# Attention heads of a conditioned sequence model: value bias moved to GpSimd, a PSUM bank for each head tile, two of four normalising products on GpSimd

## The reference

```
x1  = layernorm(x) * (scale1 + 1) + shift1
qkv = x1 @ mat_qkv_w.T + concat(q_bias, 0, v_bias)        # 16 heads of 16 columns
q   = q / max(norm(q), 1e-12) * exp(min(scale_mul, log 100))
k   = k / max(norm(k), 1e-12)
o   = softmax(q @ k.T) @ v
x   = x + (o @ proj_w.T + proj_b) * gamma1                # then a second MLP
```

## Time and profile before

| | |
|---|---|
| median of 3 runs | 3158.72 us (3158.28 to 3159.21) |
| the profiled execution's own time | 3156.91 us |
| its span in the profile | 3155.1 us |
| PE busy | 3087.0 us (98%) |
| DVE busy | 2740.4 us (87%) |
| ACT busy | 2711.8 us (86%) |
| POOL busy | 2483.4 us (79%) |

### The profile page before, as it was taken

The page is one execution under the profiler, slowest core; times in us unless marked ns, Lnnn a source line. Parts: engine busy times, 40 slices in busy tenths (PEclk is TensorE's granted clock), DMA queues, the critical chain, the costliest instruction groups (busy, mean ns, idle before and its releaser), DMA issues.

```text
span 3155.1 us, 59484 instructions
## 1 busy us (share of the span) xinstructions
PE 3087.0 (98%) x23304; PEld 2634.1 (83%) x23304; DVE 2740.4 (87%) x2985; ACT 2711.8 (86%) x4528; POOL 2483.4 (79%) x638
## 2 busy tenths in 40 slices
PE   8999999999999999999999999999999999999999
PEld 6998899895699889988389988998848998888965
DVE  2999999986499999997659999999666999999963
ACT  4999999974699999995579999999458999999845
POOL 2999999981299999996139999999416999999910
PEclk9999999999999999999999999999999999999999
DMA  5222223210222222222022222222102222222100
GB/s 180 85 84 69 84 68 96 76 56 29 69 68 83 74 91 76 83 85 66 1 80 71 86 82 77 81 78 88 46 16 79 83 82 82 75 71 81 58 14 8
DMA packets 195240, 225.70 MB, mean 72 GB/s; under 512 B 77448, under 2 KB 149640, under 8 KB 193680
## 3 DMA queue, kind: packets, MB, share of 16 engines
q1 hardware_dynamic: 194960, 221.89, 22.8%
HBM read 217.37 MB, written 4.48 MB: 70 GB/s over the span
## 4 chain that ended last, share of the span: by engine, by line
PE 65%; POOL 20%; issue 7%; ACT 4%; DVE 2%; DMA 1%; SPq 0%; DVEq 0%; POOLq 0%; ACTq 0%
PE bank L1140 17%; POOL states L680 13%; PE bank L1120 12%; PE bank L1020 9%; PE bank L1121 7%; POOL y_gated L680 6%; PE bank L1365 4%; PE bank L1116 3%; PE bank L1402 2%; PE bank L1505 2%; PE bank L1390 2%; ACT decay L865 1%; ACT inflow_tok L856 1%; PE bank L1196 1%; PE bank L1293 1%
## 5 line engine op out<-in xcount | busy, mean ns | idle before, releaser
L680 POOL TENSOR_TENSOR states<-states,c_rows 128x2048 f32<-128x2048 f32 x336 | 1532.0, 4577 | 120.5 <-DVE states L1648 118.1
L1648 DVE TENSOR_TENSOR_SCAN states<-decay,bank 128x512 f32<-128x512 f32 x1376 | 1580.6, 1202 | 38.7 <-PE bank L1121 14.2
L865 ACT ACTIVATE decay<-dt,a_log 128x512 f32<-128x512 f32 x2048 | 1309.0, 717 | 0.0
L856 ACT ACTIVATE inflow_tok<-dtx_tok,b_tok 128x512 f32<-128x512 f32 x1536 | 998.0, 719 | 62.9 <-PE bank L1121 40.2
L1120 PE MATMUL bank<-ident,inflow_tok 128*128 128x128 f32 x5280 | 898.7, 279 | 20.0 <-DVE states L1648 7.6
L1140 PE MATMUL bank<-ident,states 128*128 128x128 f32 x5504 | 826.9, 273 | 10.5 <-POOL states L680 6.2
L1648 DVE TENSOR_TENSOR_SCAN y_gated<-decay,bank 128x512 f32<-128x512 f32 x672 | 776.0, 1201 | 13.0 <-ACT decay L865 2.8
L680 POOL TENSOR_TENSOR y_gated<-y_gated,c_rows 128x2048 f32<-128x2048 f32 x168 | 768.8, 4576 | 15.7 <-DVE y_gated L1648 14.5
L1120 PEld LDWEIGHTS bank<-ident,inflow_tok 128*128 128x128 f32 x5280 | 604.6, 140 | 174.4 <-issue 60.7
L1121 PE MATMUL bank<-b_diag,dtx_tok 128*128 128x128 f32 x3520 | 680.9, 275 | 0.0
L1140 PEld LDWEIGHTS bank<-ident,states 128*128 128x128 f32 x5504 | 643.3, 141 | 21.5 <-POOL states L680 14.2
(11 more groups left out here) (174 smaller groups left out, 2583.1 us busy)
## 6 DMA issues: line engine op xcount, KB each, us to landing
c_rows<-c_spill SPq DMA_DIRECT2D x256, 512.0 KB, 3.7
b_diag<-diag_ring SPq DMA_DIRECT2D x256, 128.0 KB, 2.4
xproj_w<-in_xproj_w SPq DMA_DIRECT2D x32, 320.0 KB, 4.2
in_w<-in_in_w SPq DMA_DIRECT2D x16, 512.0 KB, 4.6
out_w<-in_out_w SPq DMA_DIRECT2D x4, 1024.0 KB, 8.3
in_w<-in_fc_w SPq DMA_DIRECT2D x8, 512.0 KB, 4.1
xproj_w<-in_w SPq DMA_DIRECT2D x8, 512.0 KB, 4.6
xproj_w<-in_fc_w SPq DMA_DIRECT2D x4, 1024.0 KB, 4.8
```

The source lines that it names most:

```text
L680: pool.tensor_tensor(state_row, state_row, c_row.to_broadcast([P, KI, L]), ALU.mult).then_inc(weighed, PAIRS)
L856: last_tok = act.activation(inflow_tok[:, r % SLOTS, t, :], dtx_tok[:, d, t, :], ACT.Copy, scale=b_tok[:, d, t, s:s + 1])
L865: act.activation(decay[:, r % SLOTS * KI + k, :], dt[:, d, k, :], ACT.Exp, scale=a_neg[:, d, k, s:s + 1]).then_inc(decay_ready, 1)
L1648: dve.tensor_tensor_scan(state_slots[r % STATES][:, k, time], decay[:, slot, time], banks[k % INFLOW_BANKS][:, time], 0.0, ALU.mult, ALU.a ...
```

## The change

- PE: the four head tiles get a bank each (4, 5, 0, 1), so no tile waits for a reader of its bank; the turns of tiles 1, 2 and 3 stand one ahead of each head tile; the bias matmuls of the values are gone.
- ACT: the squares of a tile come ahead of the copy of its keys, tile 0's stand ahead of the shift of tile 3, and keys are squared straight from PSUM as before.
- DVE: the maximum and the scale become one instruction with two tensor inputs (`norm_over`), with the inverse scale, and the reciprocal follows it; the products of tiles 2 and 3 stay on DVE.
- POOL: the products of tiles 0 and 1, and two instructions that add the value bias in place to two tiles each, once ACT has copied them; its wait for `qk_unit` ahead of L729 is gone.
- PE waits for the value bias (`v_biased`) ahead of the first product with the values.

```diff
-QK_BANK = 4
+QK_BANKS = (4, 5, 0, 1)
+POOL_TILES = 2
...
+                for t in range(POOL_TILES):
+                    pool.wait_ge(k_ready, b * TT + t + 1)
+                    pool.wait_ge(norm_inv_ready, b * TT + t + 1)
+                    pool.tensor_tensor(heads(qk_pad[:, t, :, :].rearrange("p g c -> p (g c)"), LANE)[:, :, 0:HD],
+                                       heads(qk[:, t, :], HD), norm_inv[:, t, :].unsqueeze(2).to_broadcast([P, 2 * H, HD]),
+                                       ALU.mult).then_inc(qk_unit, 1)
+                for i in range(2):
+                    values = v_ones[:, 2 * i:2 * i + 2, :, 0:HD]
+                    pool.wait_ge(v_ready, b * 2 + i + 1)
+                    pool.tensor_tensor(values, values, heads(row_b[:, V_BIAS, :], HD).unsqueeze(1).to_broadcast([P, 2, H, HD]),
+                                       ALU.add).then_inc(v_biased, 1)
                 pool.wait_ge(res_ready, (b * 2 + 1) * TT)
-                pool.wait_ge(qk_unit, (b + 1) * TT)
                 pool.tensor_tensor(proj_g, proj_w[:], gate[:, GAMMA1, :].unsqueeze(1).to_broadcast([P, KD, D]),
...
+            def square(b, t):
+                bank = banks[QK_BANKS[t]]
+                act.wait_ge(q_ready, b * TT + t + 1)
+                act.activation(qk_sq[:, t, D:2 * D], bank[:, D:2 * D], ACT.Square)
+                act.activation(qk_sq[:, t, 0:D], qk[:, t, 0:D], ACT.Square).then_inc(sq_ready, 1)
+                act.activation(qk[:, t, D:2 * D], bank[:, D:2 * D], ACT.Copy).then_inc(k_ready, 1)
...
+                square(b, 1)
+                head_root(0)
+                square(b, 2)
+                head_root(1)
+                square(b, 3)
+                head_root(2)
+                head_root(3)
...
+                ln_turn(b, 2, 1)
+                heads_tile(0)
+                ln_turn(b, 2, 2)
+                heads_tile(1)
+                ln_turn(b, 2, 3)
+                heads_tile(2)
+                heads_tile(3)
...
-                    pe.matmul(to, ident[0:1, 0:1].to_broadcast([1, P]), row_b[0:1, V_BIAS, :], start=True, stop=False,
-                              skip_group_check=True)
...
+                def invert(t):
+                    dve.wait_ge(norm_ready, b * TT + t + 1)
+                    dve.scalar_tensor_tensor(norm_over[:, t, :], norm[:, t, :], EPS_NORM, inv_scale[:], ALU.max,
+                                             ALU.mult).then_inc(norm_over_ready, 1)
+                    dve.wait_ge(norm_over_ready, b * TT + t + 1)
+                    dve.reciprocal(norm_inv[:, t, :], norm_over[:, t, :]).then_inc(norm_inv_ready, 1)
...
+                query(0)
+                query(1)
+                sum_squares(0)
+                query(2)
+                sum_squares(1)
+                invert(0)
+                query(3)
+                sum_squares(2)
+                invert(1)
+                sum_squares(3)
+                invert(2)
+                unit(2)
+                invert(3)
+                unit(3)
```

More of the change, by code:

```diff
@@ L184, in build @@
         scale_cap = sb("scale_cap", [P, H])
-        qk_scale = sb("qk_scale", [P, 2 * H])
+        inv_scale = sb("inv_scale", [P, 2 * H])
         proj_w = sb("proj_w", [P, KD, D])
@@ L249, in build @@
         norm = norm_sq
-        norm_max = norm_sq
+        norm_over = norm_sq
         norm_inv = b_diag[:, HALF + 1, :].rearrange("p (t h) -> p t h", t=TT)
@@ L294, in build @@
         cap_ready = sem("cap_ready")
-        q_scale_ready = sem("q_scale_ready")
+        inv_scale_ready = sem("inv_scale_ready")
         mod_mm = sem("mod_mm")
@@ L379, in build @@
         k_ready = sem("k_ready")
+        v_biased = sem("v_biased")
         v_ready = sem("v_ready")
@@ L383, in build @@
         norm_ready = sem("norm_ready")
-        norm_max_ready = sem("norm_max_ready")
+        norm_over_ready = sem("norm_over_ready")
         norm_inv_ready = sem("norm_inv_ready")
-        qk_inv_ready = sem("qk_inv_ready")
         qk_unit = sem("qk_unit")
+        qk_unit_high = sem("qk_unit_high")
         qk_turned = sem("qk_turned")
@@ L426, in build, with heads @@
         out_rows = out.rearrange("b (t p) d -> b p t d", p=P)
+        def heads(row, e):
+            return row.rearrange("p (h e) -> p h e", e=e)
         def lead_last(bank):
@@ L628, in _ @@
             pool.memset(ring_zeros, 0.0).then_inc(zeros_ready, 1)
-            pool.memset(qk_scale[:, H:2 * H], -1.0).then_inc(sign_ready, 1)
+            pool.memset(inv_scale[:, H:2 * H], -1.0).then_inc(sign_ready, 1)
             pool.memset(minus_half[:], -0.5).then_inc(half_ready, 1)
@@ L780, in ln @@
                 eps_of = eps[:, 0:1] if i == 1 else eps[:, 1:2]
[L781 to L787, removed]
                 root(0)
@@ L790, in ln @@
                 shift(0)
+                if i == 2:
+                    root(2)
+                    shift(1)
+                    root(3)
+                    shift(2)
+                    square(b, 0)
+                    shift(3)
+                    return
                 shift(1)
@@ L875, in _ @@
                     act.wait_ge(sign_ready, 1)
-                    act.activation(qk_scale[:, 0:H], scale_cap[:], ACT.Exp).then_inc(q_scale_ready, 1)
+                    act.activation(inv_scale[:, 0:H], scale_cap[:], ACT.Exp, scale=-1.0).then_inc(inv_scale_ready, 1)
                 prepare(0, 0, s)
@@ L906, in batch, with head_root @@
                 ln(b, 2)
-                def root(t):
+                def head_root(t):
                     act.wait_ge(norm_sq_ready, b * TT + t + 1)
                     act.activation(norm[:, t, :], norm_sq[:, t, :], ACT.Sqrt).then_inc(norm_ready, 1)
[L912 to L919, removed]
+                square(b, 1)
[5 more added lines that the diff above has]
+                head_root(3)
                 act.wait_ge(ones_ready, b + 1)
@@ L1295, in batch, with heads_tile @@
                     last.then_inc(res_mm, 1)
-                ln_turn(b, 2, 1)
-                for t in range(TT):
+                def heads_tile(t):
                     ln_wait(b, 2, t)
-                    pe.wait_ge(res_ready, (b * 2 + 1) * TT + t + 1)
                     if t > 1:
-                        pe.wait_ge(k_ready, b * TT + t - 1)
+                        pe.wait_ge(res_ready, (b * 2 + 1) * TT + t - 1)
                     for kc in range(KD):
-                        last = pe.matmul(banks[QK_BANK + t % 2], h_t[:, kc, t * P:(t + 1) * P], qkv_w[:, kc, 0:2 * D],
+                        last = pe.matmul(banks[QK_BANKS[t]], h_t[:, kc, t * P:(t + 1) * P], qkv_w[:, kc, 0:2 * D],
                                          start=(kc == 0), stop=(kc == KD - 1))
                     last.then_inc(qk_mm, 1)
-                    if t == 0:
-                        ln_turn(b, 2, 2)
-                        ln_turn(b, 2, 3)
+                ln_turn(b, 2, 1)
[5 more added lines that the diff above has]
+                heads_tile(3)
                 def value_tile(t):
                     to = banks[V_BANK + t // 2][:, t % 2 * D:(t % 2 + 1) * D]
-                    pe.matmul(to, ident[0:1, 0:1].to_broadcast([1, P]), row_b[0:1, V_BIAS, :], start=True, stop=False,
-                              skip_group_check=True)
                     for kc in range(KD):
-                        last = pe.matmul(to, h_t[:, kc, t * P:(t + 1) * P], qkv_w[:, kc, 2 * D:3 * D], start=False,
+                        last = pe.matmul(to, h_t[:, kc, t * P:(t + 1) * P], qkv_w[:, kc, 2 * D:3 * D], start=(kc == 0),
                                          stop=(kc == KD - 1), skip_group_check=True)
@@ L1328, in turn_heads @@
                         for t in range(TT):
-                            pe.wait_ge(qk_unit, b * TT + t + 1)
+                            if t < POOL_TILES:
+                                pe.wait_ge(qk_unit, b * POOL_TILES + t + 1)
+                            else:
+                                pe.wait_ge(qk_unit_high, b * (TT - POOL_TILES) + t - POOL_TILES + 1)
                             last = pe.transpose(banks[TURN_BANK + i][:, t * P:(t + 1) * P], qk_pad[:, t, i * NG + g, :], ident[:])
@@ L1396, in weigh @@
                     pe.wait_ge(probs_t_ready, b * UNITS + (j + 1) * HG)
+                    if j == 0:
+                        pe.wait_ge(v_biased, (b + 1) * 2)
                     if g and kt == 0:
@@ L1720, in sum_squares, with query @@
                                       ALU.add).then_inc(norm_sq_ready, 1)
-                def unit(t):
+                def query(t):
+                    dve.wait_ge(qk_mm, b * TT + t + 1)
+                    dve.tensor_tensor(qk[:, t, 0:D], banks[QK_BANKS[t]][:, 0:D], row_b[:, Q_BIAS, :], ALU.add).then_inc(q_ready, 1)
+                def invert(t):
                     dve.wait_ge(norm_ready, b * TT + t + 1)
[L1724 to L1733, removed]
@@ L1738, in batch @@
                     dve.wait_ge(sign_ready, 1)
[L1739 to L1748, removed]
```

(8 more changed lines are left out.)

2 lines of the change are left out of this document (1 added, 1 removed).

## The result

The changed kernel takes 3173.06 us (median of 5 runs, 3169.43 to 3179.32) against 3158.28 for the kernel before on the same chip (5 runs, 3154.53 to 3159.21): a ratio of 1.0052, 95% interval 1.004 to 1.0065. It is slower, by some 15 us. That lies inside the range of 3144 to 3176, and outside the forecast's own range of 3154 to 3165. The profiled execution took 3173.06 us, with a span of 3171.3.

A forecast was written before the change was run, and what follows sets the result against it. It took PE's chain from the MLP's residual to the first score, with DVE close behind, as the bound. PE's 3.5 us a batch less 4.1 us of waits gave +0.8 us: 3158.72 + 0.8 = 3159.5, own range 3154 to 3165, full 3144 to 3176.

The forecast's parts named there:

- rival 4: POOL beside DVE: one more POOL step lost than placed, or steps of 1.9 to 2.35 us; +7 to +17 us; chance 0.16.
- The forecast's own sum: Stretch before the first score, four batches: fair turns, POOL steps of 1.27 us; +0.8 us, giving 3159.5; chance 0.33.
- the collisions: DVE's two-input guard steps and products wait for POOL's SBUF reads: 4.1 us of waits, eating the 3.5 us gained.
- A: Stretch from tile 0's heads to the first score; last transposes forecast 0.2 us later, times four +0.8 us.
- PE's own gain: PE's heads and values before the first score: 3.5 us a batch, 2.5 from the bias matmuls, the rest the stall.
- Rivals 1 and 2: DVE beside POOL: no holding-up that matters, 3145, chance 0.15; or only large products wait, guard steps slip through, 3148, chance 0.17.
- Rival 3: POOL keeps its turn through back-to-back instructions, delaying DVE's product 3 by 13.6 us a batch; +50 us, 3209; chance 0.19.
- whole-instruction hold: A two-SBUF-input DVE instruction and a SBUF-reading POOL instruction block each other for a whole instruction; 3.10 against 0.68 us.
- PE's clock: PE's pause before the scores may shift when its clock falls: at most some 1 us a batch, +-4 us.
- B: Attention from first score to the last pair turning its output rows; 73.38 and 72.61 us before, only the clock varying it.

The follow-up runs named there:

- e1: Changed kernel plus seven spare matmuls in PE's wait ahead of the first turned heads, POOL left as it is; 3157.46 us, ratio 1.0001.
- e6: Kernel before with only the value bias moved to POOL behind all head products, plus five spare matmuls in PE's wait; 3157.62 us, ratio 1.0001.
- e4: Kernel before with only the bias matmuls removed and POOL adding the value bias behind all head products; no spare matmuls; 3175.45 us, ratio 1.0045.
- e8: Changed kernel with all four products on DVE, POOL's value bias behind them, four spare matmuls in PE's wait; 3147.05 us, ratio 0.9974.
- e2: Changed kernel with POOL's value bias held back until DVE's products of tiles 2 and 3 are done; 3151.04 us, ratio 0.9983.
- e5: Changed kernel with POOL's value bias held back behind DVE's products, plus three spare matmuls in PE's remaining wait; 3147.97 us, ratio 0.9969.

## Why the prediction came out as it did

**The range held by luck.** The time lies inside 3144 to 3176 only because rival 4 stretched the upper end to 3176, for slower or further POOL steps, and those didn't come. The forecast's own sum, with its 4 us for the clock, missed.

**Right: the collisions eat what PE gains.** The forecast said that A would change by +0.2 us a batch, +0.8 in all; it changed by +0.7. That the two numbers stand so near is luck. The waits on DVE came to 3.0 us (0, 0.61, 0.76, 1.08, 0.54) and not 4.1, in part since POOL's product takes 1.06 and not 1.27, and the guard step of tile 1 goes free; DVE's last product ended 15.11 us after tile 0's heads began, where 15.6 was forecast. Against that, in batches 0 and 3 the lower clock already caught the last transposes (1.33 in batch 0 instead of 0.77), which is why A is 17.27 and 17.11 there and 16.70 and 16.71 in the other two. With the same collisions and the clock up (e1) A sums to 66.9, 0.2 less than before the change.

**Right, but too small: PE's own gain.** Heads and values are 4.2 us shorter, not 3.5. A value tile takes 0.865 us, not 1.06, without the bias matmul in its bank, so that pair cost 1.685 - 0.865 = 0.82 us and not its own 0.62 (the four tiles took 6.74 us from 733.39 to 740.13). On the path this is worth nothing (e6, 0.2 us a batch).

**Rivals 1 and 2 fell**: guard steps of 32 columns are held too (0.79 and 1.26 for 0.18). **Rival 3 fell**: POOL's L742, L746 and L748 followed without a gap and DVE came in between each time, and POOL's next step waited for it. The whole-instruction hold that the prediction took from the Trainium skill (SBUF - State Buffer, Who interferes with whom) was there: product 3 ended 0.55 us after the POOL step beside it. Who comes next, the runs show as turn by turn. **Rival 4** gives a time near the measured one by the wrong road: POOL's steps were 1.06 and 1.27 alone, and no further one was lost.

**The term that failed is PE's clock**, put at "at most some 1 us a batch: +-4 us". It measured +4.0 to +5.6 us a batch, +18.1 in all. The bound was read from the spread between batches of one kernel, where the half-clock stretch lay late in the scores in all four batches; it said nothing of what that stretch costs when it lies at their start. The prediction itself left PE standing "in them" (the waits, 4.1 us) and reckoned that this could move the fall of the clock, but priced the move by that spread alone. That the clock is the cause is shown: PE's idleness without collisions brings the loss (e4), PE fed takes it away with collisions (e1) and without (e6, e8), and the granted clock reads 0.50 over the records that grew. That more of a later stretch costs little is in the earlier trace rows; that this is because DVE sets the pace there is argued from the windows and wasn't tried by itself.

The Trainium skill (TensorE: Matmul & The Clock Gate, HAM oscillation) tells of a kernel whose matmul bursts are parted by waits for DMAs, so that each burst starts at the lower clock. The trace agrees, with waits for DVE in place of DMAs: 2.08 us for four scores behind the waits, 1.13 without them. The prediction didn't weigh it.

**Open**: what decides where the half-clock stretch falls. With waits of 0.36 and 0.96 us (e2) B was 3.2 and 5.7 us longer than before the change in two batches, 1.1 us longer in a third, and not longer in the last. The granted clock over B stays under 1 even with PE fed (0.93 in e1, 0.95 in e5, batch 0), so such a stretch still comes, later.

## What to carry to other kernels

Work taken off an engine that then only waits gains nothing, and on TensorE it can cost. Price its idle time by what follows it: where the first matmuls behind the wait set the pace, take their records at the lower clock into the bounds (here about double, some 10 us long). A few spare matmuls in the gap bring that back, and they cost nothing where PE would stand anyway. Work that reads SBUF on GpSimd is better placed behind VectorE's chain of steps with two SBUF inputs than beside it, even if each such step is small, as long as it isn't on the path itself; here holding it back by one wait gave 2.4 us a batch.

## What the hardware showed beyond what was expected

- POOL's product of 512 elements a partition took 1.06 us with one input repeated over 16 columns (L736), and the addition to the values (L742) 1.27 us undisturbed, as L746 did. Writing 16 columns of every 32 cost nothing extra.
- DVE and POOL take turns instruction by instruction, even where POOL's queue is full: a product of 0.69 us came in between two of POOL's steps that stood back to back, and POOL's 0.73 us step became 1.18. In the earlier trace rows a POOL step still went ahead of a DVE that had asked 0.2 us before; that case didn't come up again.
- A value product without the bias matmul ahead of it took 0.865 us a tile instead of 1.06, for the same four matmul records.
